# Eighteen instead of seventeen blocks sorted for the experts, twelve expert tiles moved behind the last chunk, and a packed count

## The reference, cut to what matters

```
x1  = x + relu(adj @ (item_feat @ W_item.T + b_item) + layernorm(x) @ W_user.T + b_user)
f   = layernorm(x1)
p   = softmax(f @ gate_w + gate_b)             # 8 experts, the best two count
out = x1 + sum over the two best e of p[e] * (gelu(f @ W1[e] + b1[e]) @ W2[e] + b2[e])
```

## Time and profile before

| | us |
|---|---|
| median of 3 runs | 1459.08 (1456.51 to 1461.09) |
| the profiled execution | 1456.03 |
| its span, first to last instruction | 1454.2 |
| PE busy | 1423.4 (98%) |
| DVE busy | 1256.4 (86%) |
| ACT busy | 1095.0 (75%) |
| POOL busy | 718.1 (49%) |

### The profile page before, as it was taken

How to read it: one execution, slowest core, us unless ns; L and a number is a source line. 1 busy time by engine, 2 the same in 40 slices (tenths; PEclk the granted TensorE clock), 3 DMA queues, 4 the chain that set the end, 5 groups by cost and what they waited for, 6 DMA issues and landing times.

```text
span 1454.2 us, 20448 instructions
## 1 busy us (share of the span) xinstructions
PE 1423.4 (98%) x6682; PEld 1167.2 (80%) x6682; DVE 1256.4 (86%) x1775; ACT 1095.0 (75%) x1165; POOL 718.1 (49%) x396
## 2 busy tenths in 40 slices
PE   8999999999999999999999999999999999999898
PEld 7888888888888888888877778878888887777677
DVE  6889889889889898898898889888898988888787
ACT  5777767767767777677676878787878878787676
POOL 0024344343533542443435276877767784577730
PEclk9999999999999999999999999999999999999999
DMA  9999999999999999999999999989999999888861
GB/s 360 389 341 373 379 391 373 378 387 366 383 379 365 385 372 370 393 367 382 384 363 395 358 314 326 346 305 345 318 341 326 324 386 307 275 276 281 198 134 28
DMA packets 124711, 489.44 MB, mean 337 GB/s; under 512 B 24216, under 2 KB 29592, under 8 KB 123518
## 3 DMA queue, kind: packets, MB, share of 16 engines
q1 hardware_dynamic: 112798, 457.43, 85.1%
q0 software_dynamic: 11808, 30.71, 7.4%
HBM read 456.00 MB, written 40.99 MB: 342 GB/s over the span
## 4 chain that ended last, share of the span: by engine, by line
PE 76%; DVE 8%; issue 5%; POOL 4%; DMA 4%; ACT 3%; SPq 1%; DVEq 0%; POOLq 0%; ACTq 0%
PE p_agg L471 21%; PE p_agg L466 20%; PE p_agg L467 20%; DVE s_a_lo L925 4%; POOL rr L1351 3%; DMA s_raw<-adj 2%; PE p_hid L559 2%; PE p_hid L561 1%; PE p_hid L560 1%; ACT s_a_hi L711 1%; PE p_agg L482 1%; PE p_small L512 1%; PE p_y L575 1%; PE p_y L576 1%; PE p_y L577 1%
## 5 line engine op out<-in xcount | busy, mean ns | idle before, releaser
L925 DVE TENSOR_TENSOR s_a_lo<-s_raw,s_a_hi 128x1500 fp32r<-128x1500 f32 x520 | 881.0, 1717 | 96.4 <-PE p_agg L471 47.6
L711 ACT ACTIVATE s_a_hi<-s_raw 128x1500 fp32r<-128x1500 f32 x520 | 749.7, 1453 | 196.8 <-PE p_agg L471 176.4
L466 PE MATMUL p_agg<-s_a_hi,s_h_hi 128*128 128x500 f32 x1560 | 624.9, 401 | 0.3 <-ACT s_a_hi L711 0.2
L467 PE MATMUL p_agg<-s_a_hi,s_h_lo 128*128 128x500 f32 x1560 | 606.3, 389 | 0.0
L471 PE MATMUL p_agg<-s_a_lo,s_h_hi 128*128 128x500 f32 x1560 | 443.8, 393 | 8.9 <-DVE s_a_lo L925 8.0
L1342 POOL DMA_INDIRECT zs<-s_rows,s_idx x136 | 235.6, 1732 | 257.1 <-DVE s_idx L1083 207.1
L1351 POOL DMA_INDIRECT rr<-s_ysb,s_dests x192 | 280.0, 1458 | 158.8 <-DVE s_ysb L1164 107.2
L471 PEld LDWEIGHTS p_agg<-s_a_lo,s_h_hi 128*128 128x128 f32 x1560 | 287.3, 188 | 88.3 <-DVE s_a_lo L925 32.3
L466 PEld LDWEIGHTS p_agg<-s_a_hi,s_h_hi 128*128 128x128 f32 x1560 | 294.0, 188 | 57.7 <-issue 3.4
L467 PEld LDWEIGHTS p_agg<-s_a_hi,s_h_lo 128*128 128x128 f32 x1560 | 294.3, 189 | 56.8 <-issue 3.4
L1318 POOL TENSOR_TENSOR s_gt<-s_ebase,s_gt 125x32 f32<-125x32 f32 x20 | 128.2, 6409 | 68.7 <-DVE s_gt L1009 68.6
(11 more groups left out here) (216 smaller groups left out, 1275.9 us busy)
## 6 DMA issues: line engine op xcount, KB each, us to landing
s_raw<-adj SPq DMA_DIRECT2D x520, 750.0 KB, 6.7
s_wraw<-w SPq DMA_DIRECT2D x56, 256.0 KB, 3.0
s_zt<-zs SPq DMA_DIRECT2D x48, 264.0 KB, 3.7
out_s<-rr POOLq DMA_DIRECT2D x12, 512.0 KB, 7.1
s_xtok<-x_tok SPq DMA_DIRECT2D x20, 256.0 KB, 6.7
s_xt<-x_t SPq DMA_DIRECT2D x20, 250.0 KB, 7.5
zs<-s_early SPq DMA_DIRECT2D x18, 264.0 KB, 6.2
out_s<-s_x1s SPq DMA_DIRECT2D x17, 256.0 KB, 6.9
```

The costliest lines, as they stand in the source:

```text
L466: mm(o, h_hi[:, k * D:(k + 1) * D], hi, start=(k == 0), stop=False)
L467: mm(o, h_lo[:, k * D:(k + 1) * D], hi, start=False, stop=False)
L711: fn(a_hi[:, n % HIS, :], raw[:, n % RAW, :], ACT.Copy).then_inc(hi_made, 1)
L925: tt(a_lo[:, n % LOS, :], raw[:, n % RAW, :], a_hi[:, n % HIS, :].bitcast(F32), ALU.subtract)\
```

## The change

S becomes 18 and the groups (0 to 12) and (13 to 17): NT = 33 + 17 = 50 tiles, and two dense blocks, ND = 16 steps. The last TAIL_TILES = 12 sorted tiles are no longer spread over the chunks; they follow the last chunk one by one, and the dense steps follow them (DENSE0 = NCH + 12). So IN_STREAM = 38 tiles are left in the stream, five of them from the second group. For the twelve, the split input lies in the chunk buffers `a_hi` and `a_lo`, two deep, and the scaled output of each has a buffer of its own in `raw`, so `y_out` waits for no send there. The order within a step behind the last chunk is another too: second layer one step after the first, output transpose one after that.

The count in `prefix` uses one matmul of 32 columns in place of four of 8 that accumulate, and DVE sums over the four parts (`tot`). The adjacency's tail comes without its padding, as three loads of 17 rows. The final sums of blocks 12 to 17 are three pieces per rank instead of one of five blocks, and the last block's two powers are put between the sends.

```diff
-S = 17
-GROUPS = [(0, 12), (12, S)]
+S = 18
+GROUPS = [(0, 13), (13, S)]
...
+TAIL_TILES = 12
+PADS = 2 + TAIL_TILES
...
-STEP = [(FIRST_W1[1] - FIRST_W1[0]) / NTG[0], (NCH - 2 - FIRST_W1[1]) / NTG[1]]
-W1_AT = [FIRST_W1[g] + int(STEP[g] * i) for g in range(2) for i in range(NTG[g])]
+STEP = [(FIRST_W1[1] - FIRST_W1[0]) / NTG[0], (NCH - 2 - FIRST_W1[1]) / (NTG[1] - TAIL_TILES)]
+W1_AT = [FIRST_W1[g] + int(STEP[g] * i) for g in range(2) for i in range((NTG[0], NTG[1] - TAIL_TILES)[g])]
 NI = NT + ND
-W1_AT += [NCH + d for d in range(ND)]
-W2_AT = [w + 3 for w in W1_AT]
-YT_AT = [w + 2 for w in W2_AT[:NT]]
-ZT_AT = [w - 3 for w in W1_AT[:NT]]
+IN_STREAM = NT - TAIL_TILES
+DENSE0 = NCH + TAIL_TILES
+W1_AT += [NCH + i for i in range(TAIL_TILES + ND)]
+W2_AT = [w + (3 if w < NCH else 1) for w in W1_AT[:NT]]
+YT_AT = [w + (2 if lag(w) < NCH else 3 if w < NCH else 1) for w in W2_AT]
+ZT_AT = [w - (3 if w < NCH else 2) for w in W1_AT[:NT]]
...
+        def zhi(k):
+            return a_hi[:, k % 2, 0:T] if k > IN_STREAM else zh[:, :]
...
         def yrows(k):
-            return ysb[:, k % 2, :]
+            j = k - IN_STREAM
+            return ysb[:, k % 2, :] if j < 0 else flat[:, 4 * UB + j * T:4 * UB + (j + 1) * T]
...
-                sp.dma_start(tail_raw[:, :], adj_tail[b]).then_inc(tail_loaded, 16)
+                else:
+                    sp.wait_ge(tail_zero, 1)
+                for i in range(3):
+                    sp.dma_start(tail_raw[i * 32:i * 32 + TAIL + 1, :], adj_tail[b]).then_inc(tail_loaded, 16)
...
-                for s in range(SUBS):
-                    last = mm(small[:, o:o + E], full, mr[0:TS, s * E:(s + 1) * E],
-                              start=(s == 0), stop=(s == SUBS - 1))
-                last.then_inc(prefix_done, 1)
+                mm(small[:, o:o + SUBS * E], full, mr[0:TS, :], start=True, stop=True).then_inc(prefix_done, 1)
...
-                tt(base[:, :], base[:, :], small[:, o:o + E], ALU.add).then_inc(base_set, 1)
+                nc.vector.reduce_sum(tot[:, :], small[:, o:o + SUBS * E].rearrange("p (s e) -> p e s", e=E), AX.X)\
+                    .then_inc(tot_made, 1)
...
+                dve.wait_ge(tot_made, p + 1)
+                tt(base[:, :], base[:, :], tot[:, :], ALU.add).then_inc(base_set, 1)
...
-                if k >= 2:
+                if k >= IN_STREAM:
+                    dve.wait_ge(lo_made, NCH)
+                elif k >= 2:
                     dve.wait_ge(sent[k % 2], 16 * SUBS * (k // 2))
...
+                if n == NCH + 1:
+                    power_of_rs(BLOCKS)
+                if n == NCH + 5:
+                    power(BLOCKS - 1)
...
-                        i = k - (NT - PAIRS)
+                        i = k - NTG[0]
...
-            power_of_rs(BLOCKS)
-            power(BLOCKS - 1)
-            add_rank(PAIRS, 0)
-            add_rank(PAIRS, 1)
+            for k in range(2):
+                for i in range(PAIRS, S // 2):
+                    add_rank(i, k)
```

More of the change, by code:

```diff
@@ L64, with lag @@
 BIAS = 6
-XR = 8
+XR = 16
+def lag(n):
+    return min(n + LAG, max(n, NCH))
 FILL_AT = [(hi + 1) * CH for lo, hi in GROUPS]
@@ L419, in _ @@
                         load_zt(k)
+            for o in range(2, NT + 2):
+                if o < NT and ZT_LOAD[o] >= NCH:
+                    load_zt(o)
+                if W_LOAD[o] >= NCH:
+                    load_w(o)
             load_w(NT + 2)
@@ L692, in _ @@
                 items(n)
-                if d == 0:
+                if j == 0:
                     x1_turn(BLOCKS - 1)
                     gate_logits(BLOCKS - 1)
+                if d == -2:
+                    z_turn(S)
                 if d == 2:
                     z_turn(S + 1)
[L698 to L701, removed]
+                if j == 13:
+                    cw_turn(S + 1)
         @block.scalar
@@ L782, in z_round @@
                 act.wait_ge(turned, k + 1)
-                if k >= 1:
+                if k > IN_STREAM:
+                    act.wait_ge(chunk_used, NCH)
+                    act.wait_ge(hid_ready, k - 1)
+                elif k >= 1:
                     act.wait_ge(hid_ready, k)
@@ L786, in z_round @@
                     act.wait_ge(b2_split, 1)
-                fn(zh[:, :], tp[:, :], ACT.Copy).then_inc(zh_made, 1)
+                fn(zhi(k), tp[:, :], ACT.Copy).then_inc(zh_made, 1)
             def gelu(k):
@@ L822, in dense_gelu @@
                     act.wait_ge(lo_made, NCH)
+                if d == 1:
+                    act.wait_ge(gl_made, NT)
                 if d >= 3:
@@ L837, in items @@
             def items(n):
+                if n >= NCH:
+                    for k in range(NT):
+                        if EVAC_AT[k] == n and W2_AT[k] < n:
+                            y_evac(k)
+                    for k in range(NT):
+                        if ZR_AT[k] == n:
+                            z_round(k)
                 for k in range(NT):
@@ L840, in items @@
                         gelu(k)
+                if n >= NCH:
+                    for o in range(NT + 2):
+                        if SPLIT_AT[o] == n:
+                            w_round(o)
+                    for k in range(NT):
+                        if GELU_AT[k] == n:
+                            g_round(k)
+                    for k in range(NT):
+                        if EVAC_AT[k] == n and W2_AT[k] == n:
+                            y_evac(k)
+                    return
                 for k in range(NT):
@@ L1186, in items @@
             def items(n):
+                if n >= NCH:
+                    for k in range(NT):
+                        if ZR_AT[k] == n:
+                            ext(k)
+                            z_rest(k)
+                    for o in range(NT + 2):
+                        if SPLIT_AT[o] == n:
+                            w_rest(o)
+                    for k in range(NT):
+                        if GELU_AT[k] == n:
+                            g_rest(k)
+                    for k in range(NT):
+                        if YOUT_AT[k] == n:
+                            y_out(k)
+                    return
                 for k in range(NT):
@@ L1281, in _ @@
                     dense_out(S + (d - 3) // E - 1)
[L1282 removed]
+                if d == 3:
+                    dz_rest(S + 1)
+                if j == 1:
                     stats2(BLOCKS - 1)
                     variances(BLOCKS)
[L1285 removed]
+                if j == 4:
                     shifts(BLOCKS)
[L1287 to L1289 removed]
+                if j == 5:
                     logits(BLOCKS - 1)
[L1291 to L1292 removed]
+                if j == 8:
                     softmax(BLOCKS - 1)
[L1294 removed]
+                if j == 9:
                     top(BLOCKS - 1, 0)
[L1296 removed]
+                if j == 10:
                     top(BLOCKS - 1, 1)
[L1298 removed]
+                if j == 11:
                     mask(BLOCKS - 1)
@@ L1322, in add_rank @@
                 blocks = GROUPS[0][1] // PAIRS
-                first, last = (i * blocks, (i + 1) * blocks) if i < PAIRS else GROUPS[1]
+                first, last = i * blocks, (i + 1) * blocks
                 if k == 0:
@@ L1361, in _ @@
             pool.wait_ge(late_loaded, 16 * NL)
-            for i in range(2):
+            for i in range(PADS):
                 gp.tensor_scalar(pads[:, i, :], dest0[:, :], float(DUMP + i * T), None, ALU.add).then_inc(spare_set, 1)
@@ L1414 @@
     at = adj[:, cut:].reshape(BLOCKS, UB, TAIL).transpose(0, 2, 1)
-    tail = np.zeros((BLOCKS, TAILP, UB), np.float32)
+    tail = np.concatenate([at, np.ones((BLOCKS, 1, UB), np.float32)], 1)
     x = f("x")
@@ L1423 @@
     for r in (0, 32, 64):
-        tail[:, r:r + TAIL] = at
-        tail[:, r + TAIL] = 1.0
         feat_tail[:, r:r + TAIL] = feat[cut:].T
```

117 lines of the change are left out of this document (44 added, 73 removed).

## The result

The changed kernel takes 1484.18 us (median of 4 runs, 1482.79 to 1486.16) where the kernel before, beside it, takes 1458.12 (1456.51 to 1461.09): ratio 1.018, interval 1.016 to 1.020. It is slower by 1.8%; I had predicted 1449 (1437 to 1461). The profiled execution has a span of 1484.4 us.

The account below looks back on a forecast made before the run. PE bounds the stream, ending at 1320.3 us (1364.2 - 38.2 - 0.7 - 5.0); behind it GpSimd's sends and sums add 123, the last semaphore 1: 1444.3. Plus 1.8 and 3.0 to the runs' median: 1449 (1437 to 1461).

Parts of the forecast that it names:

- The stream's saving: Up to the last chunk's end: 38.2 us saved for tiles, 0.7 for transposes, 5.0 for the slot count.
- 5.0 for the packed count: In the stream: one 32-column matmul for four saves 0.34 us a block, less 0.8 for the eighteenth sorted block: 5.0.
- That the three tail loads cost nothing: In the stream: three tail loads instead of one come before anything waits for them, taken as 0.
- T: The stream's end, at the last adjacency chunk: forecast at 1320.3 us, against 1364.2 before.
- my 3.9 us a tile: In the stream: each tile adds 3.9 us on PE, saved in full when the tile leaves.
- PE's road, T + 110: PE behind the last chunk: twelve tiles 50.4 us, norm and gate 2, dense steps about 10 and then 47.6.
- The ring: In the tail tiles: gelu, two roundings and DVE's rest run one after another through one buffer, 4.18 us, taken as 4.2.
- the first rival: PE ends last, behind the stream: sends at 5.0 us a tile, a pass of sums 8; 1435 us, chance 0.14.
- GpSimd's road, T + 123: Behind the last chunk: 13 tiles' sends 75.4 us, sums' issues 3.9, power 5.4, then two passes; ends last, chance 0.62.
- the floor that I gave to a rival: Behind the stream: four indirect sends at 5.0 us a tile, in the case that PE ends last, chance 0.14.
- The sends' pace: Behind the last chunk: most sends 0.96 us, some 1.4 beside DVE's two-operand SBUF subtractions; 5.8 taken a tile.
- The clock rival: Twelve tile steps at 1.2 GHz: 7.6 us a tile, 1476 us; with an unseen wait 0.10, of which 0.08 slower.

Follow-up runs that it names:

- the run in the kernel before: Kernel before plus 36 indirect sends in one unbroken run beside the dense steps, to a spare part of the table: PE's end 1453.2 us instead of 1450.9.
- the sends are thinned: Changed kernel with padded tail load, sums chained pair by pair, a tiny GpSimd operation after every second send of the last nine tiles: 1454.56 us, ratio 0.997.
- border case (short pauses): Changed kernel with padded tail load; from the fourth tail tile GpSimd waits, behind a tile's first send, for the previous tile's landing: 1463.1 us (1453 to 1474).

## Why the prediction was wrong

- *The stream's saving.* 5.0 for the packed count is right (5.1 measured alone). That the three tail loads cost nothing is wrong: 8.2 us of T in the changed kernel (one profile each). I argued from their being early; the cost is in adjacency chunks that land late. Of the other 3 of the 11 the last block shows a part: 91 us, PE idle some 4 of them. Before, with more tiles, it idles as much (3.8), so that share of my 3.9 us a tile didn't leave with the tiles; the rest stays open.
- *PE's road, T + 110.* Two errors. Undisturbed it is 118 to 122. Nearly all of these 8 to 12 us lie in the twelve tile steps; from the first dense step on PE needs about 57 us, as forecast. The ring itself is the smaller part: the plain step is 4.28 where I said 4.2, but some steps wait for data that arrive late, as at 1364.17 in the changed kernel:

```profile
1342.22 0.66 PE L562 MATMUL p_tp<-s_cst,s_zt 128*128 128x128 f32 x4 [1.90 <-DMA s_zt<-zs]
1364.17 1.11 PE L562 MATMUL p_tp<-s_cst,s_zt 128*128 128x128 f32 x4 [3.73 <-DMA s_zt<-zs]
```

  The load behind the second of these rows was issued at 1355.60, 8.5 us earlier, beside the sums' traffic; before, the median of such loads is 3.7. I costed the ring by its engines and left its transfers out.
- *The step that failed*: "PE's road" was summed as if PE's signals arrive when PE ends. In 37 us of the first dense steps they came 2 to 9 us late. PE's road is 28 to 32 us longer for it (some 3 of them are the wait for weights at 1447.48), and that is no term of the sum and none of the rivals. With T and the tile steps as measured, PE's road would have given 1331.3 + 120 + 4.8 = 1456 and GpSimd's 1331.3 + 123 + 5.8 = 1460, no change; with PE's road as measured, 149.8, it is 1486 (the profiled execution: 1486.2). So PE's road ended last, as the first rival has it, but for a reason that this rival doesn't name.
- *GpSimd's road, T + 123*: right, T + 126, by two errors that cancel. A tile's sends take 5.06, the floor that I gave to a rival, not 5.8; but the last tile's wait for the late signals, and the sends end at T + 101 instead of T + 96. A pass of sums takes 11.9 (forecast 12):

```profile
1431.15 1.25 POOL L1389 DMA_INDIRECT rr<-s_raw,s_dests  x1 [0.30 <-issue]
1434.27 2.54 POOL L1371 DMA_DIRECT2D out_s<-rr  x3 [1.87 <-DMA rr<-s_raw,s_dests]
1446.12 2.38 POOL L1371 DMA_DIRECT2D out_s<-rr  x3 [9.31 <-DMA out_s<-rr]
```

- *The sends' pace.* With DVE idle, sends go at 0.96, which I took to be good for GpSimd's road alone. It makes them dense, and the damage idles DVE, which keeps them dense; beside a busy DVE (the run in the kernel before) they come 1.53 apart and delay no recorded signal. That the two feed each other fits the rows and wasn't tested by itself. The Trainium skill (SBUF — State Buffer, "SBUF: two separate sides") has GpSimd and a DVE instruction with two SBUF operands shut each other out of a shared port pair; that sends last 0.96 where DVE is idle (1400.85 to 1404.33) agrees with it.
- *The clock rival* had the right sign and nearly the size (slower, 1476) by the wrong mechanism, which is luck. The tile steps run at the upper level for most of their time (0.94). The clock falls where PE has stood idle for 3.7 to 10 us (1364.17, 1399.28, 1412.55): a consequence, and it stays up when the sends are thinned (0.996 over the span, 0.986 in the changed kernel). Its chance of 0.08 for slower was far too low for a kernel with a wholly new stage, of which the trace before shows no piece.

## What to carry to other kernels

When work is moved into a stage of its own, its engines and queues meet there at rates that no trace shows yet: give an unknown stall in it a chance of its own, and cost the transfers of its ring as well as its engines. When a consumer waits for an engine that by the profile is long done, look at what GpSimd and the DMA queues do without a break in that stretch; holding that work back for one run tells more than any reading. And a load of fewer bytes is not a cheaper load: try it alone.

## What the runs showed of the hardware

- While GpSimd issued indirect sends back to back (0.96 us each, 0.30 between), TensorE's semaphore signals came 2 to 9 us late, up to 18 in the kernel with the padded load; the recorded ones of ACT and DVE in the same stretch came on time. With 1.5 us per send beside busy dense steps, or a pause of 2.1 us or more after four to eight, they came on time but for some of 1 to 2 us. 72 plain copies in 43 us, with two pauses, didn't do it. By which path the signals are held up no run shows.
- In the border case (short pauses) one and the same program took anything from 1453 to 1474 us.
- Three 17-row loads of 33 KB beside a stream that keeps the DMA engines 99% busy cost 5.8 us over twenty blocks against one 96-row load of 188 KB. Why, no run shows.
